# Inverse of a 128-square triangular matrix by three nested products instead of four, with the work around it moved

## The chip, the cores and the metric

The kernel runs on one core of a Trainium2 chip. The metric is the device time of one execution in microseconds, the median of three runs. All data are float32. Tiles marked fp32r are float32 kept for TensorE's other float32 mode: in the trace a job of products of such tiles is 8 matmul instructions, and 16 where a plain float32 tile takes part.

## What is computed

A layer on x of shape (4, 512, 512): a bidirectional WKV mix, a gated delta rule attention with 16 key heads and 32 value heads of 128, a residual, a second mix and a feed-forward product with a binarized weight, and a residual. The change lies in the attention, which in the reference is, cut to what matters:

```python
qkv, z = conv_silu(x @ W_qkv), x @ W_z                 # per group: q, k, two v, two z
g = cumsum(g) ; decay = tril(exp(g_i - g_j))
M = stril((k * beta) @ k.T * decay)
T = solve_triangular(eye + M, eye)                     # inverse of a unit lower triangular matrix
v_c, k_cumdecay = T @ (v * beta), T @ (k * beta * exp(g))
# over chunks: attn = q @ k.T * decay; v_new = v_c - k_cumdecay @ state; out; state update
h = rmsnorm(out) * norm_w * silu(z)
y = h @ W_out.T
```

The kernel uses chunks of 128 tokens, so a sequence has four (NCH = 4), and inverts a 128 x 128 matrix for each chunk and head.

## The kernel before

A first phase (some 0.2 ms) makes the first mix and the gates. Then a loop of 66 rounds runs over 16 groups (a key head with its two value heads) times 4 sequences (b = 0 to 3), three rounds deep: in one round, `l` is the unit that makes queries, keys and the b matrix, `m` the unit whose values, z and inverse are made, `n` the unit whose chunks run through the recurrence and whose output is projected. Every engine has its own queue, written out by hand as a sequence of slots k = 0 to 19 (SLOTS), with semaphores between engines. An engine works through its queue in order.

In the first half of a round TensorE runs projections with the four hops of the recurrence in between. In the second half (slots 9 to 19, FIRST = SLOTS - JOBS = 9) it makes the inverse: eleven jobs of four products for each of two heads (`product`, L865), one job a slot, each followed by filler: the second half of the z projection (L739), `key_products` (L789), `query_tokens` (L780), `heads_t` (L819) and the eight halves of the output projection `out` (L830). Each job of a head waits for the result of the job before it, which ScalarE copies (L1124) or VectorE adds (`finish_product`, L1325 to L1331) from PSUM to SBUF; ADDED lists the jobs that VectorE finishes.

The inverse starts from the exact inverses D of the 16 x 16 diagonal blocks, which GpSimd computes a round earlier (`invert_blocks`, L1512) and SyncE scatters into `inv16`; `lower` holds the matrix with its diagonal blocks set to zero, made by GpSimd (`off_blocks`, L1488). Jobs 0 to 7 build the inverse P from powers of X = D times lower; job 8 transposes P, job 9 forms the residual against `pair`, job 10 corrects P by one Newton step.

What else the prediction follows:

- VectorE: `key_sums` (L1262, L1264: diagonal of the key products, summed), `heads` (L1293: the output times `rstd`), `gate_heads` (L1299), `query_sums` (L1269), `small` (L1275 to L1287: a dozen tiny operations, among them `edd`, L1277, whose semaphore is sk_ready, and `cpos`, L1285), `b_matrix` (first the masked key products `kks`, L1306, then L1311), `add_out` (L1388), and in round b = 1 and b = 2 of each group two scans of the second mix (L1340 with two one-element products L1342, L1343; L1350).
- ScalarE: `copy_ktok`, `silu_z`, `copy_vtok` (L1082, empties the banks ra and rb), `query_squares`, `exp_decay` with a table load, `mix_inverse` in b = 3.
- GpSimd: `mask_gates` (L1502), `rstd` (L1569, a power), in b = 0 and b = 3 a split of the weights in two halves (`w_high`, L1527; `w_low`, L1529; in b = 1 the split stands at the head of the round), `irk` (L1581, a power), `off_blocks`, parts of the mix, `invert_blocks`.
- Order before, in slots: 9 z (first half) and `key_products`; 10 `query_tokens`, `heads_t`; 11 z (second half); 12 to 18 the halves of `out`. On VectorE slot 10 holds `heads`, the scans and `key_sums`, 11 `gate_heads`, 12 `query_sums` and `small`, 13 and 15 `b_matrix`.

Of the kernel before, what the change touches and what calls it, by code (L numbers as in the profile page):

```python
# [7 lines left out]
ALU = mybir.AluOpType  # L8
# [16 lines left out]
SLOTS = 20  # L25
JOBS = 11
# [450 lines left out]
def attention_phase(nc, ctx, t):  # L477

    with ExitStack() as c:
# [30 lines left out]
        kks = sq[:, 0, :].rearrange("p (c s) -> p c s", s=CH)  # L510
# [18 lines left out]
        def halves(x):  # L529
# [30 lines left out]
                 "rstd_ready h_ready ht_full ht_ready op_full op_ready attn_ready "  # L560
# [10 lines left out]
        ADDED = (4, 6, 7, 9, 10)  # L571
# [28 lines left out]
        def _(sp):  # L600
# [40 lines left out]
            def scatter_blocks(m):  # L641
# [4 lines left out]
                if m > 0:  # L646
                    for h in range(HPG):
                        await_product(sp, m - 1, h, 4)
# [59 lines left out]
        def _(pe):  # L708
# [113 lines left out]
            def out_half(n, m, l, j, h):  # L822
# [5 lines left out]
                if (j, h) == (1, 0) and l is not None:  # L828
                    W("sk_ready", l + 1)
# [9 lines left out]
                (natural, lower),  # L839
                (s1, s0),  # L840
                (s0, s1),
                (s0, turned),
                (lower, s2),
                (s2, pinv),
                (s0, pinv),
# [54 lines left out]
            def body(l, m, n, b):  # L900
# [57 lines left out]
                for k in range(FIRST, SLOTS):  # L958
# [9 lines left out]
                    elif k == 10:  # L968
                        if L:
                            query_tokens(l, m, p)  # L970
                        if B:
                            heads_t(n, m)
                    elif k == 11:
                        proj("z", 1, 2, 3)
# [4 lines left out]
                    elif k == 14:  # L979
                        out(1, 0)  # L980
                    elif k == 15:
                        out(1, 1)
                    elif k == 16:
                        out(2, 0)
                        out(2, 1)
                    elif k == 17:
                        out(3, 0)
                    elif k == 18:
                        out(3, 1)
# [7 lines left out]
        def _(act):  # L997
# [38 lines left out]
            def exp_decay(l, h):  # L1036
# [4 lines left out]
                for ch in range(NCH):  # L1041
                    ins = a(decay[:, h, ch, :], gb[:, h, sl(ch, CH)], ACT.Exp, bias=sm["gneg"][:, ch, h:h + 1])
                ins.then_inc(S["decay_ready"], 1)
# [5 lines left out]
            def mix_scale(u, k, b):  # L1049
                W("mix_back_ready", u + 1)  # L1050
# [62 lines left out]
            def body(l, m, n, b):  # L1113
# [4 lines left out]
                for k in range(SLOTS):  # L1118
# [19 lines left out]
                    if L:  # L1138
# [10 lines left out]
                        elif k == 10:  # L1149
                            query_squares(l)  # L1150
                        elif k == 12:
                            exp_decay(l, 0)
                        elif k == 14:
                            exp_decay(l, 1)
# [13 lines left out]
                    if A:  # L1168
# [5 lines left out]
                        elif k == 11:  # L1174
                            silu_z(m, 1, q)
                            if L and 0 < l < ITERS - 1:
                                load_input((b + 1) % BATCH)
                    if L and k == 15:
                        if b == 0:
                            mix_exps(*mix_unit(l))  # L1180
                        elif b == 1:
                            mix_scale(*mix_unit(l))
# [4 lines left out]
            DEST = [s0, s1, s2, lower, pinv, s0, pinv, pinv, s1, s2, None]  # L1187
# [6 lines left out]
        def _(dve):  # L1194
# [63 lines left out]
            def key_sums(l):  # L1258
# [5 lines left out]
                v.tensor_reduce(sums[:, 0, :], work, AX.X, ALU.add)  # L1264

            def query_sums(l):

                W("squares_ready", l + 1)
                v.tensor_reduce(sums[:, 1, :], sq[:, 0, :].rearrange("p (c s) -> p c s", s=CH), AX.X, ALU.add)  # L1269

            def small(m, p):
# [4 lines left out]
                v.tensor_scalar(qe[p][:, :], sums[:, 1, :], HD * EPS, HD * EPS * HD * EPS, ALU.mult, ALU.add)  # L1276
# [13 lines left out]
            def heads(n):  # L1290
                W("rstd_ready", n + 1)
                o = oraw[:, :, :, :].rearrange("p c h e -> p (c h) e")
                v.tensor_tensor(o, o, sm["rstd"][:, :, :].rearrange("p c h -> p (c h)").unsqueeze(2).to_broadcast([P, NCH * HPG, HD]), ALU.mult).then_inc(S["h_ready"], 1)  # L1293

# [7 lines left out]
            def b_matrix(l, h, p):  # L1302

                if h == 0:
                    W("kk_full", l + 1)
                    v.tensor_tensor(kks, x0[:, :].rearrange("p (c s) -> p c s", s=CH),  # L1306
                                    t["strict"][:, :].unsqueeze(1).to_broadcast([P, NCH, CH]), ALU.mult)
                    dve.drain()
# [371 lines left out]
```

## Time and profile before

| | |
|---|---|
| median of 3 runs | 3396.2 us (3393.94 to 3398.38) |
| the profiled execution | 3396.61 us, its span 3394.8 us |
| TensorE matmul | 3187.6 us busy, 94% |
| VectorE | 2510.9 us, 74% |
| ScalarE | 1984.0 us, 58% |
| GpSimd | 1592.0 us, 47% |
| granted TensorE clock, mean | 0.993 |
| a round in the middle | about 48.2 us |

Busy time is when an engine has an instruction running. The chain is the work that ended last, followed back from the last instruction; a piece in it lasts from when what it waited for was there until the next piece takes over, so the pieces can be added. In the timeline, neighbouring rows of one engine overlap a little, because instructions are pipelined, and a row can begin before the engine gets what it needs. Times are from the start of the span.

### The profile page before, as it was taken

How to read it: one execution, taken by the hardware profiler on the slowest of the kernel's cores; microseconds unless marked ns; L12 is line 12 of the kernel's file. 1: busy time of each engine (PE TensorE's matmuls, PEld its weight loads, DVE VectorE, ACT ScalarE, POOL GpSimd, SP SyncE). 2: the span in 40 equal slices, each digit the busy share in tenths (PEclk: the TensorE clock that was granted, in tenths of full speed). 3: DMA queues.
4: the chain of work that ended last, by engine and by line, in shares of the span. 5: the costliest groups of instructions: out<-in, count | busy, mean ns of one | idle time of the engine just before them, and what ended most of it. 6: DMA issues, size and time to landing. Idle time of an engine off the chain costs nothing.

```text
span 3394.8 us, 57303 instructions
## 1 busy us (share of the span) xinstructions
PE 3187.6 (94%) x18210; PEld 2528.4 (74%) x18210; DVE 2510.9 (74%) x5359; ACT 1984.0 (58%) x4832; POOL 1592.0 (47%) x2825
## 2 busy tenths in 40 slices
PE   0149999999999999999999999999999999999999
PEld 0138787878778877887787877787878778877865
DVE  7866777777777777777777777777777777777754
ACT  6735655565566655665566556655565556656652
POOL 7653545445454544445444544545354544545330
PEclk9989999999999999999999999999999999999999
DMA  3322222222222222222232222223222222223222
GB/s 112 124 79 88 84 59 85 81 71 69 81 88 78 78 71 83 71 83 66 84 87 79 60 84 78 81 59 91 82 84 62 82 82 72 80 69 89 71 55 75
DMA packets 296750, 267.79 MB, mean 79 GB/s; under 512 B 221664, under 2 KB 251488, under 8 KB 287200
## 3 DMA queue, kind: packets, MB, share of 16 engines
q1 hardware_dynamic: 287520, 134.09, 15.9%
q10 hardware_dynamic: 8928, 130.03, 10.5%
q8 instruction: 146, 2.39, 0.3%
q14 instruction: 156, 1.28, 0.1%
HBM read 233.35 MB, written 30.67 MB: 78 GB/s over the span
## 4 chain that ended last, share of the span: by engine, by line
PE 91%; DVE 1%; issue 1%; ACT 1%; POOLq 0%; POOL 0%; DVEq 0%; ACTq 0%
PE x L739 31%; PE lane L865 20%; PE x L830 7%; PE rb L759 5%; PE ra L747 4%; PE rc L772 3%; PE rb L830 3%; PE ra L830 3%; PE rc L770 2%; PE ra L748 2%; PE rc L789 2%; PE x L789 2%; PE rb L819 1%; PE x L780 1%; PE rc L796 1%; PE x L892 1%
## 5 line engine op out<-in xcount | busy, mean ns | idle before, releaser
L739 PE MATMUL x<-xs,w_high 128*128 128x512 f32 x3072 | 1056.9, 425 | 20.7 <-DVE attn L1317 7.7
L1020 ACT ACTIVATE uvec<-rb,cpos 128x128 f32<-128x128 f32 x512 | 160.4, 364 | 847.0 <-PE rb L759 847.0
L739 PE MATMUL x<-xs,w_low 128*128 128x512 f32 x1536 | 609.5, 397 | 0.0
L739 PEld LDWEIGHTS x<-xs,w_high 128*128 128x128 f32 x3072 | 526.8, 191 | 85.7 <-issue 12.4
L1124 ACT ACTIVATE slot<-lane 128x512 fp32r<-128x512 f32 x640 | 364.7, 650 | 154.2 <-PE lane L865 154.2
L1512 POOL TENSOR_TENSOR block_step<-block_in 64x14 f32<-64x14 f32 (+6 forms) x896 | 231.4, 258 | 341.3 <-DMA block_in<-blocks_dram 220.0
L739 PEld LDWEIGHTS x<-xs,w_low 128*128 128x128 f32 x1536 | 290.3, 189 | 67.2
L1488 POOL TENSOR_TENSOR lower<-bt,offdiag 128x512 fp32r<-128x512 f32 x128 | 163.3, 1276 | 366.1 <-DVE bt L1311 366.1
L1218 DVE SCALAR_TENSOR_TENSOR cacc<-x,cwv,cacc 128x511 f32<-128x511 f32 (+2 forms) x384 | 281.6, 747 | 37.9 <-ACT cacc L1007 3.3
L1569 POOL TENSOR_TENSOR rstd<-rarg,powers 128x8 f32<-128x8 f32 x64 | 107.0, 1672 | 416.3 <-DVE rarg L1255 416.3
L1218 DVE SCALAR_TENSOR_TENSOR cacc<-x,cwqk,cacc 128x511 f32<-128x511 f32 (+2 forms) x384 | 281.2, 746 | 28.0 <-ACT cacc L1007 6.1
L1514 POOL TENSOR_TENSOR block_in<-block_in,block_step 64x14 f32<-64x14 f32 (+6 forms) x896 | 238.5, 266 | 131.1 <-issue 5.9
L830 PE MATMUL x<-vT,w_out 128*128 128x512 f32 x512 | 275.3, 620 | 1.2 <-DVE vT L1299 1.2
L865 PE MATMUL lane<-pinv,slot 128*128 128x128 f32 x1536 | 270.9, 319 | 1.1 <-ACT slot L1124 0.9
L865 PEld LDWEIGHTS lane<-pinv,slot 128*128 128x128 f32 x1536 | 203.2, 193 | 92.1 <-issue 58.8
L1244 DVE SCALAR_TENSOR_TENSOR wvec<-ra,egn,vtok 128x128 f32<-128x128 f32 x384 | 117.0, 346 | 172.9 <-PE ra L748 172.9
L1581 POOL TENSOR_TENSOR irk<-skt,powers 128x4 f32<-128x4 f32 x64 | 64.6, 1009 | 353.6 <-PE x L739 353.3
L1327 DVE TENSOR_TENSOR pinv<-lane,pinv 128x512 fp32r<-128x512 f32 x256 | 164.4, 683 | 27.0 <-PE lane L865 27.0
L1029 ACT ACTIVATE junk<-oraw 128x128 f32<-128x128 f32 x512 | 159.0, 311 | 41.8 <-DVE oraw L1238 3.1
L1502 POOL TENSOR_TENSOR gb<-gb,causal 128x512 f32<-128x512 f32 x128 | 165.9, 1296 | 18.5
L1293 DVE TENSOR_TENSOR oraw<-oraw,rstd 128x1024 f32<-128x1024 f32 x64 | 128.9, 2015 | 60.1 <-POOL rstd L1569 60.1
L1325 DVE TENSOR_TENSOR pinv<-lane,inv 128x512 fp32r<-128x512 f32 x128 | 82.4, 686 | 119.7 <-PE lane L865 119.7
(299 smaller groups left out, 7460.0 us busy)
## 6 DMA issues: line engine op xcount, KB each, us to landing
xs<-mix_dram ACTq DMA_DIRECT2D x62, 2048.0 KB, 7.7
gb<-cum_dram SPq DMA_DIRECT2D x128, 256.0 KB, 4.3
w_in<-in_w_qkvz SPq DMA_DIRECT2D x48, 512.0 KB, 4.1
w_out<-in_w_out SPq DMA_DIRECT2D x16, 512.0 KB, 5.8
blocks_dram<-bt SPq DMA_DIRECT2D x512, 8.0 KB, 1.5
inverse_dram<-block_out SPq DMA_DIRECT2D x64, 128.0 KB, 2.2
inv<-inverse_dram SPq DMA_DIRECT2D x512, 16.0 KB, 1.9
xacc<-in_x SPq DMA_DIRECT2D x4, 1024.0 KB, 10.1
```

What stands on the lines that cost most here:

```text
L739: ins = mm(PROJ_BANK[kind][i][:, :], w, x, start=(k == 0 and j == 0), stop=(k == KC - 1 and j == 2))
L759: ins = mm(rb[:, sl(h, HD)], pair[p][:, h, ch, :], rhs, start=True, stop=True)
L830: ins = mm(OUT_BANK[j][:, :], w_out[:, h, sl(j, P)], hT[:, h, :], start=(h == 0), stop=(h == HPG - 1))
L865: ins = mm(lane[h][:, sl(ch, CH)], a, b, start=True, stop=True)
L1020: ins = a(uvec[:, h, :], rb[:, sl(h, HD)], ACT.Copy, scale=sm2[p]["cpos"][:, ch, h:h + 1])
L1124: a(DEST[job][:, h, :, :].rearrange("p c s -> p (c s)"), lane[h][:, :], ACT.Copy).then_inc(copied[h], 1)
L1218: ins = v.scalar_tensor_tensor(out=cacc[:, i, j:SEQ], in0=PROJ_BANK[kind][i][:, 0:SEQ - j], scalar=weights[:, i, 3 - j:4 - j], in1=cacc[:, ...
L1327: ins = v.tensor_tensor(pinv[:, h, :, :], made, pinv[:, h, :, :], ALU.add)
L1488: ins = g.tensor_tensor(lower[:, h, :, :], pair[p][:, h, :, :], t["offdiag"][:, :].unsqueeze(1).to_broadcast([P, NCH, CH]), ALU.mult)
L1502: g.tensor_tensor(x, x, t["causal"][:, :].unsqueeze(1).to_broadcast([P, NCH, CH]), ALU.add).then_inc(S["masked"], 1)
L1512: g.tensor_tensor(step, block_in[:, 0:i, i:i + 1].to_broadcast(shape), block_in[:, i:i + 1, i + 1:BLK].to_broadcast(shape), ALU.mult)
L1514: g.tensor_tensor(block_in[:, 0:i, i + 1:BLK], block_in[:, 0:i, i + 1:BLK], step, ALU.add)
```

## The change

Three parts.

**The inverse.** Ten jobs instead of eleven, in nineteen slots instead of twenty. With P = (I + X) D, made by job 2, and X2 = X X by job 3, jobs 4, 5 and 6 form P + X2 (P + X2 (P + X2 P)), each a product with X2 and a sum with P. Before, two squarings of X (jobs 2 and 3), P by job 4, and three more products (5, 6, 7). VectorE now finishes six jobs (2, 4, 5, 6, 8, 9), ScalarE copies four (0, 1, 3, 7); before five and six.

**Order.** On TensorE, slot 10 now holds `heads_t` and the second z half, slot 11 `query_tokens`; the halves of `out` are in slots 12 to 17, with both of `out(1)` in 14 and both of `out(2)` in 15. The first half of `out(1)` waits for squares_ready instead of sk_ready. On VectorE, slot 10 holds one scan (b = 1, 2), `key_sums`, which now also makes `kks`, and `small`; slot 11 `gate_heads` and then the sum for job 2; slot 12 `query_sums` with `qe`; slots 14 and 15 `b_matrix`; slot 16 two `add_out` and the other scan. On ScalarE the exponentials of both heads stand together in slot 12, `exp_small` in 13, `silu_z` for the second half in 10, `query_squares` in 11, `mix_scale` in 17.

**Heads.** The product of the output with `rstd` goes from VectorE to GpSimd, behind the power that makes `rstd` and ahead of the weight split.

```diff
@@ -22,8 +22,8 @@
...
 BLK = 16
-SLOTS = 20
-JOBS = 11
+SLOTS = 19
+JOBS = 10
@@ -507,7 +507,7 @@
...
 block_out = sb("block_out", [NB * HPG * NCH, 2, BLK, BLK], F32R)
-kks = sq[:, 0, :].rearrange("p (c s) -> p c s", s=CH)
+kks = sq[:, 1, :].rearrange("p (c s) -> p c s", s=CH)
...
@@ -568,7 +568,7 @@
...
-ADDED = (4, 6, 7, 9, 10)
+ADDED = (2, 4, 5, 6, 8, 9)
...
@@ -826,7 +826,7 @@
...
         if (j, h) == (1, 0) and l is not None:
-            W("sk_ready", l + 1)
+            W("squares_ready", l + 1)
@@ -837,12 +837,11 @@
...
         (natural, lower),
+        (s0, turned),
         (s1, s0),
-        (s0, s1),
-        (s0, turned),
-        (lower, s2),
         (s2, pinv),
-        (s0, pinv),
+        (s2, s0),
+        (s2, s1),
@@ -966,26 +965,25 @@
...
             elif k == 10:
+                if B:
+                    heads_t(n, m)
+                proj("z", 1, 2, 3)
+            elif k == 11:
...
                     query_tokens(l, m, p)
-                if B:
-                    heads_t(n, m)
-            elif k == 11:
-                proj("z", 1, 2, 3)
...
                 out(1, 0)
+                out(1, 1)
             elif k == 15:
-                out(1, 1)
-            elif k == 16:
...
                 out(2, 1)
+            elif k == 16:
+                out(3, 0)
             elif k == 17:
-                out(3, 0)
-            elif k == 18:
@@ -1033,21 +1031,22 @@
...
-    def exp_decay(l, h):
+    def exp_decay(l, h, chunks):
...
         W("masked", 2 * l + h + 1)
-        for ch in range(NCH):
+        for ch in chunks:
             ins = a(decay[:, h, ch, :], gb[:, h, sl(ch, CH)], ACT.Exp, bias=sm["gneg"][:, ch, h:h + 1])
-        ins.then_inc(S["decay_ready"], 1)
+        if NCH - 1 in chunks:
+            ins.then_inc(S["decay_ready"], 1)
...
     def mix_scale(u, k, b):
-        W("mix_back_ready", u + 1)
+        W("mix_back_ready", 2 * u + 2)
@@ -1146,12 +1145,12 @@
...
                     silu("qk", l, 1, qkT2[p][:, 0, :])
-                elif k == 10:
+                elif k == 11:
...
                 elif k == 12:
-                    exp_decay(l, 0)
-                elif k == 14:
-                    exp_decay(l, 1)
+                    exp_decay(l, 0, range(NCH))
+                    exp_decay(l, 1, range(NCH))
+                elif k == 13:
@@ -1171,20 +1170,20 @@
...
                     copy_vtok(m)
-                elif k == 11:
+                elif k == 10:
...
                         load_input((b + 1) % BATCH)
+            if L and k == 17 and b == 1:
+                mix_scale(*mix_unit(l))
...
                     mix_exps(*mix_unit(l))
-                elif b == 1:
-                    mix_scale(*mix_unit(l))
...
     s0, s1, s2 = slot
-    DEST = [s0, s1, s2, lower, pinv, s0, pinv, pinv, s1, s2, None]
+    DEST = {0: s0, 1: s1, 3: s2, 7: s1}
@@ -1262,18 +1261,22 @@
...
         v.tensor_reduce(sums[:, 0, :], work, AX.X, ALU.add)
-
-    def query_sums(l):
+        dve.drain()
+        v.tensor_tensor(kks, x0[:, :].rearrange("p (c s) -> p c s", s=CH),
+                        t["strict"][:, :].unsqueeze(1).to_broadcast([P, NCH, CH]), ALU.mult)
+
+    def query_sums(l, p):
...
         v.tensor_reduce(sums[:, 1, :], sq[:, 0, :].rearrange("p (c s) -> p c s", s=CH), AX.X, ALU.add)
+        dve.drain()
+        v.tensor_scalar(qe[p][:, :], sums[:, 1, :], HD * EPS, HD * EPS * HD * EPS, ALU.mult, ALU.add)
...
         v.tensor_scalar(skt[:, :], sums[:, 0, :], HD * EPS, None, ALU.add)
-        v.tensor_scalar(qe[p][:, :], sums[:, 1, :], HD * EPS, HD * EPS * HD * EPS, ALU.mult, ALU.add)
@@ -1286,11 +1289,6 @@
...
         dve.drain()
-
-    def heads(n):
-        W("rstd_ready", n + 1)
-        o = oraw[:, :, :, :].rearrange("p c h e -> p (c h) e")
-        v.tensor_tensor(o, o, sm["rstd"][:, :, :].rearrange("p c h -> p (c h)").unsqueeze(2).to_broadcast([P, NCH * HPG, HD]), ALU.mult).then_inc(S["h_ready"], 1)
@@ -1301,11 +1299,6 @@
...
-        if h == 0:
-            W("kk_full", l + 1)
-            v.tensor_tensor(kks, x0[:, :].rearrange("p (c s) -> p c s", s=CH),
-                            t["strict"][:, :].unsqueeze(1).to_broadcast([P, NCH, CH]), ALU.mult)
-            dve.drain()
@@ -1321,34 +1314,31 @@
...
             made = lane[h][:, :].rearrange("p (c s) -> p c s", s=CH)
-            if job == 4:
+            if job == 2:
                 ins = v.tensor_tensor(pinv[:, h, :, :], made, turned[:, h, :, :], ALU.add)
-            elif job in (6, 7):
-                ins = v.tensor_tensor(pinv[:, h, :, :], made, pinv[:, h, :, :], ALU.add)
-            elif job == 9:
+            elif job in (4, 5, 6):
+                dst = {4: s0, 5: s1, 6: pinv}[job]
+                ins = v.tensor_tensor(dst[:, h, :, :], made, pinv[:, h, :, :], ALU.add)
+            elif job == 8:
...
-    def mix_backward(u, k, b):
-
-        dve.drain()
+    def mix_backward(i, u, k, b):
+
...
         decays = t["dec"][:, 1, k, b:b + 1]
-        for x in (mix_e[:, 0, ::-1], mix_q[:, ::-1]):
-            v.tensor_tensor_scan(x, decays.to_broadcast([P, SEQ]), x, 0.0, ALU.mult, ALU.add)
-        dve.drain()
-        v.tensor_tensor(mix_first[:, 0:1], mix_e[:, 0, 0:1], decays, ALU.mult)
-        v.tensor_tensor(mix_first[:, 1:2], mix_q[:, 0:1], decays, ALU.mult).then_inc(S["mix_back_ready"], 1)
-
-    def mix_forward(u, k, b):
-
-        dve.drain()
+        x = (mix_e[:, 0, ::-1], mix_q[:, ::-1])[i]
+        v.tensor_tensor_scan(x, decays.to_broadcast([P, SEQ]), x, 0.0, ALU.mult, ALU.add)
+        dve.drain()
+        v.tensor_tensor(mix_first[:, i:i + 1], (mix_e[:, 0, 0:1], mix_q[:, 0:1])[i], decays, ALU.mult).then_inc(S["mix_back_ready"], 1)
+
+    def mix_forward(i, u, k, b):
+
         W("mix_scaled_ready", u + 1)
-        for i, x in enumerate((mix_e[:, 0, :], mix_q[:, :])):
-            ins = v.tensor_tensor_scan(x, t["dec"][:, 1, k, b:b + 1].to_broadcast([P, SEQ]), x, mix_first[:, i:i + 1], ALU.mult, ALU.add)
-        ins.then_inc(S["mix_forward_ready"], 1)
+        x = (mix_e[:, 0, :], mix_q[:, :])[i]
+        v.tensor_tensor_scan(x, t["dec"][:, 1, k, b:b + 1].to_broadcast([P, SEQ]), x, mix_first[:, i:i + 1], ALU.mult, ALU.add).then_inc(S["mix_forward_ready"], 1)
@@ -1402,7 +1392,7 @@
...
                 add_out(n, 3)
-            if A and k - FIRST in ADDED:
+            if A and k - FIRST in ADDED and k - FIRST > 2:
@@ -1411,11 +1401,11 @@
...
                     norm_out(n, p)
-                elif k == 10:
-                    heads(n)
...
             if A:
+                if k - FIRST == 2:
+                    finish_product(m, 2, 1 - p)
@@ -1439,19 +1429,27 @@
...
                     if b == 1:
-                        mix_backward(*mix_unit(l))
+                        mix_backward(0, *mix_unit(l))
                     elif b == 2:
-                        mix_forward(*mix_unit(l))
+                        mix_forward(0, *mix_unit(l))
                     key_sums(l)
+                    small(l, p)
                 elif k == 12:
-                    query_sums(l)
-                    small(l, p)
-                elif k == 13:
+                    query_sums(l, p)
+                elif k == 14:
...
                     b_matrix(l, 1, p)
-            if B and k in (15, 16, 17):
-                add_out(n, {15: 0, 16: 1, 17: 2}[k])
+            if B and k == 15:
+                add_out(n, 0)
+            elif B and k == 16:
+                add_out(n, 1)
+                add_out(n, 2)
+            if L and k == 16:
+                if b == 1:
+                    mix_backward(1, *mix_unit(l))
+                elif b == 2:
+                    mix_forward(1, *mix_unit(l))
...
@@ -1545,7 +1543,7 @@
...
-        pool.wait_ge(S["mix_forward_ready"], u + 1)
+        pool.wait_ge(S["mix_forward_ready"], 2 * u + 2)
@@ -1567,7 +1565,10 @@
...
             g.tensor_tensor(sm["rstd"][:, :, :].rearrange("p c h -> p (c h)"), sm["rarg"][:, :, :].rearrange("p c h -> p (c h)"),
-                            t["powers"][:, 0, :], ALU.pow).then_inc(S["rstd_ready"], 1)
+                            t["powers"][:, 0, :], ALU.pow)
+            pool.drain()
+            o = oraw[:, :, :, :].rearrange("p c h e -> p (c h) e")
+            g.tensor_tensor(o, o, sm["rstd"][:, :, :].rearrange("p c h -> p (c h)").unsqueeze(2).to_broadcast([P, NCH * HPG, HD]), ALU.mult).then_inc(S["h_ready"], 1)
...
                 split("v", l // BATCH)
```

## Rows read from the trace of the kernel before

**Rows 1.** Busy time by stretch: engine, (instructions), granted clock, DMA share; ten rounds.

```profile
1500.00:1984.00 484.00, 483.66 (x2812) 385.92 (x2812) 364.18 (x806) 290.33 (x737) 233.51 (x429) 1.00 0.27 78
```

**Rows 2.** Chain that ended last: start, us, what; round b = 0, last row b = 3.

```profile
1560.05 0.84 PE lane L865 x8
...
1564.96 0.46 PE x L780 x4
...
1565.86 0.51 PE rb L819 x4
1566.37 0.98 PE lane L865 x8
...
1568.79 0.84 PE lane L865 x8
1569.63 1.04 PE x L830 x2
1570.66 0.84 PE lane L865 x8
1571.50 0.91 PE x L830 x2
...
1576.76 1.77 PE ra L830 x4
...
1580.35 1.78 PE lane L865 x16
...
1532.00 2.05 PE lane L865 x16
```

**Rows 3.** Timeline of ScalarE, same round b = 0: start, us, instruction.

```profile
1564.72 0.94 ACT L1082 ACTIVATE vtok<-rb,irk 128x256 f32<-128x256 f32 x2
```

**Rows 4.** Timeline of TensorE's key products and of VectorE, same round.

```profile
1562.17 1.05 PE L789 MATMUL x<-qkT 128*128 128x128 f32 x8
...
1563.78 0.68 DVE L1262 TENSOR_TENSOR cacc<-x,ident 128x512 f32<-128x512 f32 x1
...
1565.90 0.75 DVE L1299 SCALAR_TENSOR_TENSOR vT<-ra,normw,gate_z 128x512 f32<-128x512 f32 x1 [0.68 <-PE ra L819]
...
1568.12 0.16 DVE L1277 TENSOR_TENSOR edd<-glast,gct 128x8 f32<-128x8 f32 x1
...
1568.99 0.18 DVE L1287 TENSOR_SCALAR cneg<-cpos 128x8 f32<-128x8 f32 x1
1571.10 1.29 DVE L1325 TENSOR_TENSOR pinv<-lane,inv 128x512 fp32r<-128x512 f32 x2 [1.92 <-PE lane L865]
```

**Rows 5.** Timeline of GpSimd, same round.

```profile
1559.25 1.67 POOL L1569 TENSOR_TENSOR rstd<-rarg,powers 128x8 f32<-128x8 f32 x1 [4.53 <-DVE rarg L1255]
1560.89 1.89 POOL L1527 TENSOR_TENSOR w_high<-w_in,ones 128x1024 fp32r<-128x1024 f32 x1
1562.92 3.17 POOL L1529 TENSOR_TENSOR w_low<-w_in,w_high 128x1024 fp32r<-128x1024 f32 x1
```

**Rows 6.** Same round on VectorE; then two lines' durations (min/median/max) over all rounds.

```profile
1560.95 2.91 DVE L1293 TENSOR_TENSOR oraw<-oraw,rstd 128x1024 f32<-128x1024 f32 x1 [0.94 <-POOL rstd L1569]
...
L1293 DVE TENSOR_TENSOR oraw<-oraw,rstd x64: 1224/1226/2911, 308.6 to 3355.5; 128x1024 f32<-128x1024 f32 x64
...
L1529 POOL TENSOR_TENSOR w_low<-w_in,w_high x47: 2345/3173/3195, 218.3 to 3140.7; 128x1024 fp32r<-128x1024 f32 x47
```

**Rows 7.** Timeline of GpSimd and VectorE, the first round b = 1.

```profile
254.76 2.05 POOL L1502 TENSOR_TENSOR gb<-gb,causal 128x512 f32<-128x512 f32 x1
255.82 1.01 DVE L1342 TENSOR_TENSOR mix_first<-mix_e,dec 128x1 f32<-128x1 f32 x1
```

**Rows 8.** Timeline of GpSimd and VectorE, a later round.

```profile
461.05 1.01 POOL L1581 TENSOR_TENSOR irk<-skt,powers 128x4 f32<-128x4 f32 x1 [8.06 <-PE x L739]
461.10 0.17 DVE L1285 TENSOR_TENSOR cpos<-bct,rk 128x8 f32<-128x8 f32 x1
```

**Rows 9.** Timeline of SyncE: the eight transfers that fill inv16 for the round b = 0.

```profile
1550.19 3.77 SPq L651 DMA_DIRECT2D inv<-inverse_dram  x8
```

More of the change, by code:

```diff
@@ L559, in attention_phase @@
                  "kq_full w_ready oq_ready u_full u_ready os_full s_ready o_ready ss_ready rarg_ready "
-                 "rstd_ready h_ready ht_full ht_ready op_full op_ready attn_ready "
+                 "h_ready ht_full ht_ready op_full op_ready attn_ready "
                  "mix_loaded mix_clipped mix_exp_ready mix_products_ready mix_back_ready mix_scaled_ready mix_forward_ready mix_den_ready "
@@ L647, in scatter_blocks @@
                     for h in range(HPG):
-                        await_product(sp, m - 1, h, 4)
+                        await_product(sp, m - 1, h, 2)
                 for a in range(NB):
@@ L1486, in off_blocks @@
                     if m is not None:
-                        pool.wait_ge(prod_full[h], JOBS * m + 6)
+                        pool.wait_ge(prod_full[h], JOBS * m + 2)
                     ins = g.tensor_tensor(lower[:, h, :, :], pair[p][:, h, :, :],
```

## Prediction

> **What bounds the kernel now.** I read the busy shares by stretch first: in ten steady rounds TensorE works 483.66 of 484 us at the full clock, 2.4 GHz, VectorE 364, GpSimd 234 [rows 1]. So inside a round there is next to nothing to win from the other engines; a round gets shorter only by matmul time that goes, and longer by any wait that is put in front of TensorE. Next I read the chain that ended last through the second half of one round, the one whose job 1 starts at 1564.12 (b = 0) [rows 2]; everything below is told in its times. The reader is to see that the chain is TensorE's own pieces laid end to end, and that a few are longer than their twins: those are the waits. Then the same stretch on ScalarE, VectorE and GpSimd [rows 3 to 5], to see what must be done before each piece, and last what happens where these two overlap [rows 6 to 8].
>
> **The product that goes.** A job is 8 matmuls, 0.84 us on the chain [rows 2]. One of eleven goes: -0.84 a round. Three small things go with it. Job 2 took 0.98 because it stood right behind the transposes while ScalarE still copied job 1's result: -0.14, since the z half now lies between. The first half of `out` took 1.04 against 0.91, waiting for the silu of z: -0.13. And four halves of `out` in a row at 1.77 for two cost 0.05 less than 2 x 0.91: -0.05. Together -1.16.
>
> **Heads' transposes moved ahead.** `heads_t` writes the bank that ScalarE's `copy_vtok` empties. That copy ends at 1564.72 + 0.94 = 1565.66 and the second half of `heads_t` begins a moment later, its four matmuls taking 0.51 where four others take 0.46 [rows 2, 3]. It already waits for ScalarE; from the end of a producer to the next matmul I read 0.25 to 0.3 us and use 0.28. ScalarE's work up to there is untouched (its queue holds the same calls up to slot 9). So without the query transposes (0.46) ahead of it, `heads_t` does not end sooner than 1566.37; TensorE idles 0.46 there, and pays the 0.46 of `query_tokens` later: +0.46.
>
> **A short slot in front of job 3.** Old slots between two products that need VectorE held about 0.9 us of filler. The new jobs 2 and 3 have only `query_tokens` between. From 1566.37: z half 1.44 (between jobs 2 and 3 of rows 2), job 2 at 1567.81 to 1568.65, queries to 1569.11. VectorE can add head 0 from 0.44 after a job's start and both heads take 1.29 (1571.10 against 1570.66, rows 2 and 4): head 1 is ready at 1568.25 + 1.29 + 0.28 = 1569.82, wanted at 1569.53. +0.28. The next slots hold 0.91 or 1.77 and need 0.7 to 0.8: no wait. So far a round gains 1.16 - 0.46 - 0.28 = **0.42 us**, x 64 = 26.9 us. In rounds b = 3 ScalarE's `mix_inverse` delays a copy (the residual takes 2.05 instead of 1.78 [rows 2]); that wait stays within 0.1 us, since ScalarE has lost a copy ahead of it: nothing counted.
>
> **Heads scaled on GpSimd.** This takes 1.23 us (alone) from VectorE, which has 120 us to spare in ten rounds, so it gains nothing there. On GpSimd it stands between `rstd` and the weight splits. The row that is nearest in form is L1527, 1024 elements times one repeated value: 1.89; the other end is the two-stream L1529 at its least, 2.35 [rows 5, 6]. I take 1.89. `rstd` ends at 1560.92, a drain is 0.14, the product ends 1562.95 to 1563.4; `heads_t` wants it by about 1564.9. Hidden, with 1.5 us in hand; if GpSimd took over 3.8 us it would be paid in full.
>
> **What it collides with.** VectorE and GpSimd hold each other up when VectorE reads two tensors of SBUF. The scaling took 1.22 alone, but 2.91 in 30 of 64 rounds, where GpSimd's split had begun 0.06 before it: it ended 1.08 after the split did. In return L1529 took 3.17 instead of 2.35 [rows 5, 6]. Size doesn't help: a product of one element, 0.16 alone, took 1.01, until GpSimd's 512-wide sum ended [rows 7]. Now put the new order on the b = 0 and b = 3 rounds, which have a split. GpSimd: scaling 1561.06 to 1562.95, L1527 to 1564.80, L1529 1564.94 to 1567.29. VectorE: the key products end at 1563.22 [rows 4], `key_sums` is now three operations of 0.75 with their drains, so `small` comes at 1565.5, and its difference `edd` (glast and gct, both in SBUF) at 1565.57: in the middle of L1529. It ends at 1567.31 instead of 1565.73. From the end of `edd` to the end of `small` is 0.95 (1568.28 to 1569.17 and a drain), then `gate_heads` 1.33: VectorE reaches job 2's sum at 1569.59. Without the block it would be there at 1568.0 and wait for job 2 at 1568.25. So job 3 starts **1.34 us** later. Before, `small` came at 1567.97, when the split was over [rows 4, 5]: the change moves it from behind `query_sums` to ahead of it, just into the split that the scaling has pushed back. 30 rounds x 1.34 = +40.2 us. With 2.35 for the scaling it is 1.80 and 54. Everything behind job 3 on VectorE (the sums of squares, the b matrix) moves along; the block inverses have room: the last transfer of `inv16` is issued at 1553.96 for a job 0 at 1560.05 [rows 2, 9], against some 2 us that the matrix comes later.
>
> **The scans parted.** In b = 1 and 2 one scan (about 1.25) stays in slot 10, ahead of the key products, where VectorE is idle, and one goes behind the sums of `out` in slot 16. There job 8's sum is due 0.15 us before TensorE wants it: hidden, with no margin. If it spoils, 0.3 us in 32 rounds: 10 us. In b = 1 the one-element product behind the first scan is blocked until the scaling ends, at 1563.0, before the key products: free at 1.89, some 0.1 at 2.35.
>
> **The sum.** Profiled execution 3396.6 (span 3394.8), 0.4 above the median of the runs, which I ignore. 3396.6 - 26.9 + 40.2 = **3409.9 us**, 0.4% slower.
>
> **A rule weighed.** One operation doesn't fit the picture: VectorE's `cpos`, also of two tensors in SBUF, ran in its usual 0.17 inside GpSimd's 1.01 us power `irk` [rows 8], and so in 21 rounds; a power does not hold VectorE up, at least not throughout. The Trainium skill, page "SBUF — State Buffer", section "Who interferes with whom", says that the shared pair is an exclusive lock, held for the whole instruction, by any GpSimd instruction that reads SBUF against a VectorE one with two SBUF inputs. Rows 6 and 7 agree with it; rows 8 do not.
>
> **Rivals.** (a) *Powers block too.* Then in b = 1 the first scan waits for `rstd` (1560.0 to 1560.92), ends at 1562.0, the scaling behind it at 1563.9, the one-element product last, and the key sums start 0.7 late, 0.5 more than the room at job 3: +8 us, **3418**. Against it: rows 8. 0.07. That is what the rule quoted from the Trainium skill gives here.
> (b) *GpSimd's scaling at 2.35 or a little above.* For it: two streams of 1024 cost that; against: one operand is a repeated value. 3396.6 - 26.9 + 54 + 2 = 3426, with 2.55 **3434**. 0.15.
> (c) *The small difference is not blocked*, as `cpos` is not, or it slips in between two GpSimd instructions. Then only the 0.42 remains: **3370**, faster. It decides at a block of 26.9 / 30 = 0.90 us a round: with `edd` done before 1566.9 the kernel is no slower. For it: rows 8; against: rows 7, one case in sixteen, but to the hundredth. 0.20.
> (d) *TensorE is all that counts*: all 1.16 is kept and no wait appears, 3396.6 - 74 = **3322**. It needs ScalarE to empty the bank sooner, and nothing moves it [rows 3]. 0.05.
>
> **How the numbers follow.** Forecast 3410, chance 0.53, its own range 3398 to 3424 (0.2 us a round in the 0.42, 0.1 in the 1.34). Low 3366 takes in (c), high 3436 takes in (a) and (b); outside are (d) and some edges, about 0.15. The time can be told from no change beyond 0.2%, 6.8 us. Slower: 0.43 of the forecast, 0.15 of (b), 0.06 of (a), together 0.64. Within: 0.09 of the forecast, 0.01 of (a), 0.03 of (c), 0.13. Faster: 0.01, 0.17 of (c), 0.05 of (d), 0.23.
>
> **What would show it.** In the changed profile: in b = 0 and 3 `edd` takes about 1.75 us and ends with L1529; job 3's piece of the chain is preceded by 1.3 to 1.6 us of wait for VectorE there and by about 0.3 in the other rounds; `heads_t` waits for `vtok` about 0.46; rounds b = 1, 2 are 0.4 shorter and b = 0, 3 about 0.9 longer than before. Wrong if `edd` keeps 0.16, if GpSimd's scaling is far from 1.9, or if TensorE waits at `h_ready` or job 9.

## The result, and the profile after

| | before | after |
|---|---|---|
| median | 3395.1 us (4 runs, 3393.1 to 3398.4) | 3447.6 us (4 runs, 3445.6 to 3450.0) |
| ratio, 95% interval | | 1.0154 (1.0138 to 1.0169) |
| profiled span | 3394.8 us | 3444.5 us |
| mean granted clock | 0.993 | 0.984 |

The change makes the kernel 1.5% slower: 52 us, where 13 were forecast. The direction was right, and the time lies 12 us above the range. Ten steady rounds, in the columns of [rows 1], now read so:

```profile
1500.00:1984.00 484.00, 473.61 (x2678) 372.95 (x2677) 360.65 (x797) 271.70 (x690) 245.07 (x436) 0.99 0.26 77
```

TensorE is idle 10.4 us of 484 instead of 0.3, and its clock is no longer 1.00. The chain of one round b = 0 shows both; it answers to [rows 2].

```profile
1578.59 0.84 PE lane L864 x8
1579.44 0.09 issue
1579.53 0.63 PE ra L819 x4
...
1580.17 0.66 PE rb L819 x4
1580.83 1.41 PE x L739 x6
...
1583.58 0.74 DVE vT L1297
1584.32 0.61 DVEq L1272
1584.93 0.04 issue
1584.97 1.26 PE lane L864 x8
1586.23 1.79 PE x L830 x2
1588.02 1.60 PE lane L864 x8
1589.62 0.94 PE x L830 x2
```

Job 3 (1584.97) is reached through VectorE's `gate_heads` (L1297), not through TensorE: VectorE was late. Behind it two matmul pieces have double their usual length: half of `out` takes 1.79 (0.91 in [rows 2]) and a job 1.60 (0.84). The windows over the same stretch say why (columns as in [rows 1]):

```profile
1582.00:1584.00 2.00, 1.52 (x13) 1.24 (x12) 1.66 (x6) 1.04 (x2) 1.01 (x1) 1.00 0.28 53
1584.00:1586.00 2.00, 1.03 (x8) 0.95 (x8) 2.00 (x4) 0.48 (x2) 0.00 (x0) 1.00 1.01 359
1586.00:1589.00 3.00, 3.00 (x12) 1.97 (x10) 0.47 (x3) 2.97 (x6) 0.00 (x0) 0.52 1.02 427
```

TensorE idles in the first two windows at a granted clock of 1.00; in the third it is busy all the time and has a clock of 0.52, so nearly all of it at 1.2 GHz instead of 2.4. VectorE and GpSimd in this round, answering to [rows 4] to [rows 6]:

```profile
1573.71 1.67 POOL L1567 TENSOR_TENSOR rstd<-rarg,powers 128x8 f32<-128x8 f32 x1 [1.56 <-DVE rarg L1254]
1575.52 1.90 POOL L1571 TENSOR_TENSOR oraw<-oraw,rstd 128x1024 f32<-128x1024 f32 x1
1577.38 1.90 POOL L1525 TENSOR_TENSOR w_high<-w_in,ones 128x1024 fp32r<-128x1024 f32 x1
1579.42 2.38 POOL L1527 TENSOR_TENSOR w_low<-w_in,w_high 128x1024 fp32r<-128x1024 f32 x1
...
1579.27 0.69 DVE L1265 TENSOR_TENSOR cacc<-x,strict 128x512 f32<-128x512 f32 x1
1580.03 1.79 DVE L1279 TENSOR_SCALAR skt<-sums 128x4 f32<-128x4 f32 x1
1581.73 0.15 DVE L1280 TENSOR_TENSOR edd<-glast,gct 128x8 f32<-128x8 f32 x1
1582.91 0.75 DVE L1297 SCALAR_TENSOR_TENSOR vT<-ra,normw,gate_z 128x512 f32<-128x512 f32 x1
1584.24 1.28 DVE L1318 TENSOR_TENSOR pinv<-lane,inv 128x512 fp32r<-128x512 f32 x2
```

The block is there, one instruction earlier than forecast: not `edd` but the operation ahead of it, `skt`, four elements and a constant, takes 1.79 instead of 0.17 and ends at 1581.82, 0.02 after the weight split (1581.80). Everything behind it comes late as forecast. Over the loop, TensorE's waits for this sum (what waited, what for, us in total, times, longest):

```profile
PE lane L864 <- DVE pinv L1318: 44.6, 32, 1.8
```

Read one by one, TensorE idles 1.44 to 1.46 us ahead of job 3 in 28 of the 30 steady rounds b = 0 and 3, and 1.81 in the other two.

The last view is a table of rounds, worked out from the trace: from one job 1 to the next (b is the round in which the stretch begins), parted by how long the granted clock stood at half in it. The first and the last rounds of the loop, which are not like the others, are left out of the means.

| round | before | after, clock full | after, 3.4 us at half | after, 6.8 us at half |
|---|---|---|---|---|
| b = 0 | 48.08 | 49.11 (2 rounds) | 50.81 (10) | 52.46 (3) |
| b = 1 | 48.12 | 47.62 | | |
| b = 2 | 48.06 | 47.61 | | |
| b = 3 | 48.42 | 49.45 (8) | 50.81 (7) | |
| after the last job 1 | 89.5 | 94.0, one fall in it | | |

At full clock the rounds are what was forecast (b = 1, 2: -0.50 and -0.45 for -0.42; b = 0, 3: +1.03 for +0.92). Two things are not in the forecast: 20 of these 30 rounds b = 0 and 3 have a fall of the clock, which begins 0.1 to 1.9 us after job 3 does, at 1.4 to 1.7 us for each 3.4 us of half clock, and the end of the kernel is 4.5 us longer.

### The profile page after: what moved, and what is told of

The parts are those of the page before. It is cut to its first block, busy times and chain, and to the rows that moved or that the text cites. A ratio compares the mean times of both kernels' runs of the same rounds, so it can differ in the third digit from the quotient of the medians.

```text
span 3444.5 us, 56263 instructions
## 1 busy us (share of the span) xinstructions
PE 3183.9 (92%) x17698; PEld 2489.9 (72%) x17698; DVE 2549.2 (74%) x5423; ACT 1878.9 (55%) x4576; POOL 1690.6 (49%) x2889
## 3 DMA queue, kind: packets, MB, share of 16 engines
q14 instruction: 156, 1.28, 0.1%
## 4 chain that ended last, share of the span: by engine, by line
PE 86%; DVE 3%; issue 2%; DVEq 1%; ACT 1%; POOLq 1%; POOL 0%; SPq 0%; DMA 0%
PE x L739 29%; PE lane L864 17%; PE x L830 7%; PE rb L759 5%; PE ra L747 4%; PE ra L830 3%; PE rb L830 3%; PE rc L772 3%; PE rc L770 2%; PE ra L748 2%; PE x L789 2%; PE rc L789 1%; PE rb L819 1%; PE ra L819 1%; PE x L891 1%
## 5 line engine op out<-in xcount | busy, mean ns | idle before, releaser
L1123 ACT ACTIVATE slot<-lane 128x512 fp32r<-128x512 f32 x512 | 295.6, 641 | 252.3 <-PE lane L864 252.2
L864 PE MATMUL lane<-slot 128*128 128x128 f32 x1536 | 266.3, 313 | 45.5 <-DVE pinv L1318 45.0
L1217 DVE SCALAR_TENSOR_TENSOR cacc<-x,cwqk,cacc 128x511 f32<-128x511 f32 (+2 forms) x384 | 281.2, 746 | 28.3 <-ACT cacc L1005 6.4
L864 PEld LDWEIGHTS lane<-slot 128*128 128x128 f32 x1536 | 205.7, 195 | 127.0 <-issue 53.4
L1321 DVE TENSOR_TENSOR slot<-lane,pinv 128x512 fp32r<-128x512 f32 x256 | 166.7, 687 | 135.7 <-PE lane L864 135.6
L864 PEld LDWEIGHTS lane<-pinv,slot 128*128 128x128 f32 x1024 | 150.9, 212 | 69.8 <-issue 43.6
L864 PE MATMUL lane<-pinv,slot 128*128 128x128 f32 x1024 | 199.2, 342 | 0.5 <-DVE slot L1323 0.4
L464 PE MATMUL gate<-wba,mixed 128*128 128x64 f32 x128 | 28.3, 422 | 146.4 <-DVE mixed L389 146.4
```

The source lines that it names most:

```text
L864: ins = mm(lane[h][:, sl(ch, CH)], a, b, start=True, stop=True)
L1123: a(DEST[job][:, h, :, :].rearrange("p c s -> p (c s)"), lane[h][:, :], ACT.Copy).then_inc(copied[h], 1)
L1217: ins = v.scalar_tensor_tensor(out=cacc[:, i, j:SEQ], in0=PROJ_BANK[kind][i][:, 0:SEQ - j], scalar=weights[:, i, 3 - j:4 - j], in1=cacc[:, ...
L1321: ins = v.tensor_tensor(dst[:, h, :, :], made, pinv[:, h, :, :], ALU.add)
```

## The experiments

Two theories stood against each other. **Wait and clock:** the prediction's block and waits are right, and an idle stretch of some 1.45 us on TensorE brings its clock down behind it. **Wait alone:** the wait costs more than its length for another reason, such as the transfers that run in the same stretch (DMA share 1.01 and 1.02 in the windows above) or the new order of the jobs. Beside them the parts of the sum were to be measured one by one. Unless it is said otherwise, an edit is to the changed kernel and ratios are to the kernel before, run on the same chip (its medians there were 3394.7 to 3395.9). All computation stays; the runs that fill or lengthen a wait do a piece of it again.

### The tiny operations after job 4's sum

```diff
 key_sums(l)
-small(l, p)
...
+elif k == 13:
+    small(l, p)
```

> The changed kernel with one thing moved: VectorE's `small` goes from slot 10 to slot 13, behind job 4's sum, when GpSimd's split is over. Theory A (the split blocks `small`, job 3 waits 1.5 us for it in the rounds b = 0 and 3, and TensorE's granted clock falls to half for 3.4 us behind some of these waits): no block, no such wait, no half clock; each of 64 rounds 0.42 to 0.48 us shorter than before the change, 3395 - 27 to 31, so about 3366 (3360 to 3373). Theory B (the clock falls because of the new mix of work in the second half, or because of the wait at `heads_t`): the falls stay, about 3366 + 40 = 3406.

Measured: 3379.3 us, ratio 0.9953 (0.9938 to 0.9967), and no fall of the clock in the steady rounds. So the place of `small` decides the sign of the whole change: 68 us. It came 13 us short of what was expected. Rounds b = 1 and 2 took 48.10 and 47.92 instead of 47.6: in slot 13 `small` pushes VectorE's queue back, and the sum for job 8 comes late behind the scan of slot 16.

```profile
1617.88 1.21 DVE L1333 TENSOR_TENSOR_SCAN mix_q<-dec,mix_q 128x512 f32<-128x512 f32 x1
1619.16 0.16 DVE L1335 TENSOR_TENSOR mix_first<-mix_q,dec 128x1 f32<-128x1 f32 x1
1619.24 1.28 DVE L1323 TENSOR_TENSOR slot<-lane,slot 128x512 fp32r<-128x512 f32 x2
...
1619.32 0.61 DVE slot L1323
1619.98 1.26 PE lane L864 x8
```

The last two lines are the chain: job 9 takes 1.26 instead of 0.84. That is the "no margin" of the prediction's scan step, spoiled by 0.3 to 0.5 here.

### The wait filled with work

```diff
-for ch in range(NCH):
+for ch in list(range(NCH)) * (4 if b in (0, 3) else 1):
     ins = nc.tensor.transpose(x1[:, sl(ch, HD)], qkT2[p][:, 1, sl(ch, CH)], ident[:, :])
```

The query transposes, which stand ahead of job 3, are made four times in b = 0 and 3. TensorE works where it waited, and nothing else changes.

> The changed kernel with work in the wait: in rounds b = 0 and 3 TensorE makes the four query transposes four times over instead of once (1.3 us more matmul, the same values written again), between jobs 2 and 3, where it waits 1.5 us for VectorE. The wait for VectorE itself is as long as it was. Theory A: the clock doesn't fall, and of 3447.6 the 42 us go that 85 us at half clock cost: about 3406 (3400 to 3412). If the half clock cost nothing and waits alone made the 52 us: no change, 3447. Theory B: the falls stay, 3447.

Measured: 3413.9 us, ratio 1.0059 (1.0044 to 1.0074). TensorE's wait is gone, and with it every fall:

```profile
PE lane L864 <- DVE pinv L1318: 1.6, 6, 0.5
...
1623.00:1625.00 2.00, 2.00 (x13) 1.33 (x11) 1.22 (x2) 1.97 (x5) 0.00 (x0) 1.00 0.99 426
```

The rounds take 49.18 (b = 0) and 49.41 (b = 3), what they took in the changed kernel at full clock, and the transfers are as dense (0.99). So neither the transfers nor the job order makes the rest; the clock alone costs 3447.6 - 3413.9 = **33.7 us**. What stays, 3413.9, is the forecast of 3409.9 and some 4 us; the expectation of 3406 was 8 too low: it took 42 us for the falls, half of their 85.

### The wait in part

Two more fillings, with the transposes made two and three times.

> The changed kernel with the query transposes made twice in b = 0 and 3: the wait in front of job 3 is about 1.0 us instead of 1.46. The moment at which job 3 starts is the same, so any difference from 3447 is the clock. If a wait of 1.0 us brings it down less often: between 3414 and 3447; if not at all, 3414.

> As the run before with the transposes made three times: wait about 0.55 us. The run with heads on VectorE waits 0.6 there and has no fall in these rounds, so 3414 here too.

Measured: 3414.4 and 3415.0 us (ratios 1.0053 and 1.0057), like four times. The rows are TensorE's waits for the sum of job 2, twice first:

```profile
PE lane L864 <- DVE pinv L1318: 31.5, 33, 1.4
...
PE lane L864 <- DVE pinv L1318: 18.2, 31, 0.9
```

In b = 0 and 3 the waits are 0.99 to 1.02 us long with the transposes made twice (two are 1.37 and 1.38), and 0.56 to 0.59 with three times (two are 0.9). None of them brought a fall. In the changed kernel waits of 1.44 to 1.46 brought one in 18 of 28 rounds and the two of 1.81 in both. So the length of a wait does not decide alone: of 15 waits of 1.44 us in b = 3, seven brought a fall and eight did not.

### The wait put into the kernel before

```diff
 W("squares_ready", l + 1)
-v.tensor_reduce(sums[:, 1, :], sq[:, 0, :].rearrange("p (c s) -> p c s", s=CH), AX.X, ALU.add)
+for again in range(6 if l % BATCH in (0, 3) else 1):
+    dve.drain()
+    v.tensor_reduce(sums[:, 1, :], sq[:, 0, :].rearrange("p (c s) -> p c s", s=CH), AX.X, ALU.add)
```

This is the kernel before, with its eleven jobs and its old order; VectorE sums the squares of the queries six times, ahead of its first sum of a product.

> The kernel before the change, with nothing of the change: only VectorE makes its sum of the query squares six times over instead of once in rounds b = 0 and 3 (3.75 us more; the same values). It has about 1.9 us to spare there, so job 4's sum comes 1.8 us late and TensorE waits about 1.5 us for it in 31 rounds. Price of the wait alone: 3395 + 46 = 3441. If such a wait also brings the clock down, as in the changed kernel (20 falls of 3.4 us or more in 30 rounds, 1.7 us each or more): about 3475 to 3485.

Measured: 3515.7 us, ratio 1.0355 (1.0325 to 1.0385).

```profile
PE lane L865 <- DVE pinv L1327: 49.5, 31, 1.9
...
1626.00:1629.00 3.00, 3.00 (x10) 1.97 (x10) 1.84 (x6) 2.26 (x6) 1.00 (x1) 0.50 0.26 112
...
1625.56 1.74 PE lane L865 x8
1627.30 1.81 PE x L830 x2
```

A wait of 1.6 us (49.5 / 31), and right behind it half of `out` at 1.81: the clock is 0.50 with a DMA share of only 0.26. There are 28 falls, 130 us at half clock. A round b = 0 takes 50.08 with no fall, 51.70 with one of 3.4 us, 53.21 with two; b = 1 and 2 keep 48.08 and 48.06. So a wait of that length costs 2.0 us a round by itself (one round alone gives this for b = 0; two rounds b = 3 give the same), 31 x 2.0 = 62 us. The other 58 of the 120 measured are left for the clock, somewhat less than half of the 130. That is 31 us above the upper end of what was expected: the wait costs 62 and not 46, and 28 of the 31 waits brought a fall, ten of them a double one. The mechanism is shown in both directions: filled, it goes; put into the old kernel, it comes.

### The scaling back on VectorE

```diff
-pool.drain()
-g.tensor_tensor(o, o, ..., ALU.mult).then_inc(S["h_ready"], 1)
...
+def heads(n):
+    W("rstd_ready", n + 1)
+    v.tensor_tensor(o, o, ..., ALU.mult).then_inc(S["h_ready"], 1)
```

> The changed kernel with the scaling of the heads back on VectorE in slot 10, the rest as changed. Theory A: in b = 0 and 3 the scaling is blocked by the first half of the split and ends about 1.0 us after it, but `small` then comes when the second half is over; VectorE reaches job 2's sum 0.35 us late instead of 1.34: job 3 waits about 0.6 in these rounds, too short for the clock to fall in most: 3395 - 29 + 10 = 3376 (3368 to 3386). If the cost lay in the wait at `heads_t` ahead of the z half, which this leaves as it is: still about 3447.

Measured: 3381.7 us, ratio 0.9963 (0.995 to 0.9976).

```profile
1551.75 2.91 DVE L1296 TENSOR_TENSOR oraw<-oraw,rstd 128x1024 f32<-128x1024 f32 x1 [0.94 <-POOL rstd L1574]
...
1556.86 0.17 DVE L1279 TENSOR_SCALAR skt<-sums 128x4 f32<-128x4 f32 x1
...
PE lane L864 <- DVE pinv L1323: 12.4, 34, 0.8
```

Here the split starts 1.9 earlier, as before the change; `heads` overlaps it (2.91, as in [rows 6]), and `skt` comes when it is over and keeps 0.17. The wait is 0.31 to 0.33 in most of these rounds (12.4 / 34 = 0.36 over all), and no clock falls in the steady rounds. This shows the second half of the mechanism: it takes the scaling on GpSimd **and** the early `small` to make the block; either one alone leaves the kernel faster than before.

### The old order on TensorE, with the new inverse

```diff
 elif k == 10:
-    heads_t(n, m)
-    proj("z", 1, 2, 3)
+    query_tokens(l, m, p)
+    heads_t(n, m)
 elif k == 11:
-    query_tokens(l, m, p)
+    proj("z", 1, 2, 3)
```

With `small` in slot 13 as above, and ScalarE's `query_squares` and `silu_z` in their old slots.

> As the first of these (`small` in slot 13), and TensorE's slots 10 and 11 in the order before the change: query transposes, heads' transposes, then job 2 and the second z half. By the terms of the prediction this takes back the 0.46 idle at `heads_t` and the 0.28 in front of job 3, and gives back 0.14 and 0.13 of the small waits: 0.42 + 0.46 + 0.28 - 0.27 = 0.89 us a round, 3395 - 57 = 3338 (3330 to 3348). If the new order were worth something in itself, it would be above the first run's 3366.

Then with `small` in slot 12 instead, behind `query_sums`, where it stood before:

```diff
 elif k == 12:
     query_sums(l, p)
+    small(l, p)
```

> As the fourth run (TensorE's slots 10 and 11 in the old order), but with `small` in slot 12 behind `query_sums`, where it stood before the change, not in slot 13. In slot 13 it pushed VectorE's queue back until job 8's sum came 0.3 to 0.5 us late in the rounds with a scan in slot 16. If that is so: all rounds at about 47.2 us, 3351 - 12 = 3339 (3333 to 3345). If slot 12 only moves the delay to job 4's sum: 3351 or above.

Measured: 3351.0 us, ratio 0.987 (0.9853 to 0.9886), and 3335.1 us, ratio 0.9824 (0.9807 to 0.984). The first has again the late sum in b = 1 and 2 (47.65 and 47.47 against 47.17 in b = 0), which was not expected to stay, and misses 3338 by 13 us; the second, expected at 3339, has 47.1 to 47.2 in three of the four rounds and 47.4 in b = 3. A round loses **0.96** against the kernel before, on average. The move of `heads_t` and z therefore costs 3379.3 - 3351.0 = 28.3 us, 0.44 a round; the prediction's steps for it, +0.46 and +0.28 less 0.14 and 0.13, give 0.47.

### The end of the kernel

The chain of the changed kernel behind the last job 7:

```profile
3373.01 1.80 PE lane L864 x16
...
3375.43 1.22 DVE qkT L1366
3376.65 1.14 DVE bt L1366
3377.79 0.60 DVE xacc L1378
3378.38 0.61 DVE bt L1325
3378.99 0.69 issue
3379.68 1.19 PE rb L759 x4
```

`ffn_base` (L1366), a piece of the feed-forward product, stands in slot 17, which was ScalarE's job before and is now between VectorE's sums for jobs 8 and 9. TensorE has nothing else left there and waits.

```diff
-elif k == 17:
+elif k == 16:
     ffn_base(1, 0)
```

> As the run before, and in the last round with work for the inverse the feed-forward's two VectorE products (2.4 us) go from slot 17 to slot 16. In slot 17 they now stand between the sums of jobs 8 and 9, where before the change slot 17 held a job of ScalarE's; TensorE waits 4 us for them once. Expected 4 us below the run before, 3335; if the wait is needed for something else, the same as that.

Measured on top of the kernel above: 3331.1 us, ratio 0.9811 (0.9797 to 0.9826), and 88.65 us after the last job 1 instead of 92.19: 3.5 us.

### Two edits on top that move nothing

The kernel with the end mended, and the scaling on VectorE as in the edit above:

> As the run before with the scaling of the heads on VectorE. In b = 0 and 3 the first half of the split blocks it and VectorE reaches job 2's sum 0.7 us later, about when it is needed: the same as the run before within 4 us, so that scaling on GpSimd brings nothing. If VectorE's time mattered by itself (1.2 us a round): 10 us or more slower.

Measured: 3328.7 us, ratio 0.9806 (0.9791 to 0.9821), the fastest of all, though not to be told from 3331.1. The same kernel with both scans in slot 10, as before the change, and none in slot 16:

> As the second run of this call, with both scans of a round in slot 10, as before the change. Lock theory: GpSimd's scaling, held up by the first scan, gets in before the second, which is then blocked 1.9 us; VectorE reaches job 2's sum 1 us late in b = 1 and 2: +0.45 in 32 rounds, about 3349. If the second scan goes first: no difference, 3335.

Measured: 3331.8 us, ratio 0.9813: a miss by 17 us. The block that was expected is there, and hidden. GpSimd and VectorE in a round b = 2:

```profile
1624.76 1.90 POOL L1568 TENSOR_TENSOR oraw<-oraw,rstd 128x1024 f32<-128x1024 f32 x1
...
1624.85 2.89 DVE L1341 TENSOR_TENSOR_SCAN mix_q<-dec,mix_first,mix_q 128x512 f32<-128x512 f32 x1
...
1627.66 0.66 DVE L1261 TENSOR_TENSOR cacc<-x,ident 128x512 f32<-128x512 f32 x1
```

The second scan takes 2.89 instead of 1.2 and ends at 1627.74, 1.08 after the scaling. The key sums, which could begin with the first bank of the key products at 1626.97, begin 0.7 late. In the same round of the kernel with parted scans VectorE then idles 0.42 ahead of `gate_heads`, waiting for `heads_t`, and the z half lies between job 2 and job 3 as well: these take the 0.7 up. Job 2 and job 3 follow each other here as there (job 3 comes 4.65 us after job 1, there 4.64). The expectation had counted the delay from the front of VectorE's queue and not from what the queue waits for next. So the parting of the scans, like the scaling on GpSimd, brings nothing that can be measured with this order.

## Why the prediction was right or wrong

**The product that goes, jobs 2 and `out`.** Right, and 0.08 short. With the old order the round loses 0.96. The chains of a round show where it goes: 0.84 for the job and 0.05 for the four halves of `out` in a row, as listed, and 0.08 that was not on the list, since the job behind the next four halves takes 0.84 for 0.92. Job 2 still takes 0.98 and the first `out` 1.04 there. In the changed kernel, with z between, job 2 is 0.84 and `out` 0.91, as listed.

**`heads_t` for 0.46.** Right in size, wrong in looks: in the chain above it costs 0.09 of issue and pieces of 0.63 and 0.66 for 0.46 and 0.51, together 0.42 more, but TensorE's list of waits has next to nothing for `vtok` (0.3 us in all). The wait shows on the weight loads ahead of these products, where the second half stands idle for ScalarE's copy:

```profile
1580.17 0.42 PEld L819 LDWEIGHTS rb<-ident,oraw 128*128 128x128 f32 x4 [0.25 <-ACT vtok L1081]
```

**The short slot ahead of job 3, +0.28.** Right. In rounds b = 1 job 3's piece is 1.14 for 0.84:

```profile
1633.83 0.46 PE x L780 x4
1634.29 1.14 PE lane L864 x8
1635.43 0.91 PE x L830 x2
```

**GpSimd's scaling at 1.89.** Right: 1.897 to 1.902 in all 64.

```profile
L1571 POOL TENSOR_TENSOR oraw<-oraw,rstd x64: 1897/1899/1902, 302.9 to 3405.3; 128x1024 f32<-128x1024 f32 x64
```

**The block.** Right in place and rounds, near in size (+1.34 forecast; the rounds come out 1.03 longer where 0.92 was forecast; against the rounds without a block, 49.11 for 47.6, it costs 1.5), wrong by one instruction. The prediction held that VectorE is held up when it reads two tensors of SBUF; `skt` reads one. (The scan above reads two, one of them a repeated value like `rstd` in [rows 6], and fits.) The trace of before had one such case, at 219.70 in its first round, where `skt` took 0.95 inside a split:

```profile
L1275 DVE TENSOR_SCALAR skt<-sums x64: 169/170/953, 219.7 to 3253.9; 128x4 f32<-128x4 f32 x64
```

`edd` keeps 0.15, so the prediction's own sign for "wrong" came true although its mechanism was at work: the sign was tied to one name, where it should have been tied to the group `small`. The Trainium skill, page "SBUF — State Buffer", section "Who interferes with whom", says that `tensor_scalar` can also take the pair that VectorE shares with GpSimd. The trace agrees, with `skt` at 1.79 for 0.17. Rival (c), no block, is out; so is (b), with the scaling at 1.9, and (d), since rounds b = 1 and 2 gained 0.5 and not 1.16. Against (a), that powers block too, stand the scans that began while GpSimd's power ran: all 31 of the changed kernel took their usual 1.21 to 1.28. One, from the run with both scans in slot 10:

```profile
1575.90 1.65 POOL L1564 TENSOR_TENSOR rstd<-rarg,powers 128x8 f32<-128x8 f32 x1 [1.75 <-DVE rarg L1254]
...
1576.58 1.22 DVE L1333 TENSOR_TENSOR_SCAN mix_e<-dec,mix_e 128x512 f32<-128x512 f32 x1
```

**What failed: the sum.** The step is "30 rounds x 1.34 = +40.2 us": it priced the wait in front of job 3 at its own length, once, and put what the wait does to the granted clock at nothing, without a word on it. That holds while the clock stays. In the changed kernel some 1.45 us of idle are followed by 3.4 or 6.8 us at half clock in 20 of 30 rounds. By the table of rounds, ten falls at 1.70, three double ones at 3.35 and seven in b = 3 at 1.36 make 37 us in the profiled execution; the filled kernel gives 33.7 for the median. None of the rivals had it. The trace of before had falls up to 0.28 ms, where the loop begins, and then a single one, in one of the loop's last rounds, at 3285.92; the prediction did not ask what TensorE had been doing ahead of it. It had idled 0.7, 0.7 and 0.75 us and stood in a stretch of 1.68 when the clock fell. The same stretches stand in that round of the changed kernel, and there no fall came.

**The missed term.** The last rounds were not looked at. The jobs moved one slot while `ffn_base` kept its number, and a slot that held ScalarE's job now holds VectorE's: the end is 4.5 us longer. With the old order on TensorE, moving it back gave 3.5. The end of the changed kernel also has a fall of 6.8 us in it, whose share was not measured by itself.

The account, in the profiled spans: b = 1 and 2 gave -18, 3.4 of it in the first round of the loop (forecast -13), b = 0 and 3 without falls +29 (+27.6), the start -2.4, the falls +37 (none), the end +4.5 (none): +50, measured +49.7. That the filled kernel lands within 4 us of the forecast is in part luck: the terms that it missed, about -4 in rounds b = 1 and 2, +5 in b = 0 and 3 and +3 at the end, partly cancel. The range failed for the same reason: its upper end took the block's bounds, and no mechanism that adds to a wait.

## What to carry to other kernels

In a kernel whose TensorE works without a gap, price a new wait at its length **and** ask what it does to the clock: here 1.45 us of idle cost up to 1.7 more behind a single fall, and 3.35 behind a double one. If a wait can't be avoided, work in place of it is worth trying first; a part of the wait filled was enough here. Splitting a wait into shorter ones was not tried. And take the parts of a change one by one: this inverse was worth 1.9% with TensorE's old order, `small` behind `query_sums` and the end mended, and the places that came with it turned that into a loss of 1.5%; when job numbers shift, look at everything that is tied to a slot by number, in the last rounds too.

## What was not expected of the hardware

- TensorE's granted clock went from 2.4 to 1.2 GHz behind idle stretches of 1.44 to 1.81 us (20 of 30 rounds of the changed kernel) and 1.50 to 1.90 us (28 of 31 in the kernel before with a wait put in), and stayed down for 3.4 or 6.8 us each; with stretches of 1.0, 0.6 and 0.3 us at the same place it never fell, nor with two of 1.37 and 1.38. In a late round of the changed kernel two stretches of 1.68 and 2.01 us brought none. TensorE was busy 97.9% of the time over ten rounds. What exactly the chip goes by is not settled by these runs.
- A VectorE operation that reads a single tensor in SBUF was held up by GpSimd's split: a constant added to 4 elements took 1.32 to 2.08 us in 31 rounds, mostly 1.79, for 0.17. The masked product of `key_sums`, one tensor from SBUF and one from PSUM, had begun 0.15 before the split and overlapped it, and neither took longer (0.69; 2.38 for 2.35).
- A scan over 512 elements, which reads its tensor and a repeated value, took 2.89 us for 1.2 behind GpSimd's scaling; scans that began while GpSimd's power ran took their usual time, 31 of 31.
